# Key norms read off the gram's diagonal on GpSimd, with x loaded into the tile of the gated products and the gram's load issued later

## The chip, the cores and the metric

The kernel runs on one core of one Trainium2 chip. The metric is the time of one execution on the device, in microseconds.

## The reference

A gated delta rule over 16 heads of size 16, then a layer norm, a gated feed-forward network and another layer norm. Batch 8, length 2048, width 256, hidden 768.

```python
x_act = jnp.tanh(x)
static_out = jnp.einsum('bld,ed->ble', x_act, W)
q = k = to_heads(x_act); v = to_heads(static_out)
# per head and token, with lam = sigmoid(lam_logit), beta = eta * (1 - lam) / d:
S = lam * S
u = beta * (v_t - S^T k_t)
S = S + k_t u_t^T
o = S^T q_t
...
y = layernorm(static_out + o) * ln_gamma + ln_beta
x = layernorm(x + y)
x = layernorm(x + (silu(x @ wg.T) * (x @ wu.T)) @ wd.T)
```

Since q is k, the output of a token holds the term (k_t . k_t) u_t: the squared norm of each head's key times the update. These squared norms, one for each token and head, are what the text calls the key norms. They are scaled and shifted (beta times a constant, minus a constant) into the tile nb.

## The kernel before

The 2048 tokens of each batch row are cut into 32 chunks of 64 tokens (NS = 32). A chunk holds 4 windows (NW = 4) of 16 tokens (C = 16); with the 8 batch rows a window fills 128 partitions. The recurrence over the state runs window by window. Within a window it is done with matrices: the rest R = V - K S, then the update U = T R with T the inverse of a triangular matrix made from the gram K K^T, then the new state from K^T U. Each window is therefore a chain of three matmul groups (`pe_products`, line 182) with short VectorE and ScalarE steps between them: L361, L366, L372 make the rest, L377 and L382 the update, L388, L393, L399 the state.

The order of all work is written by hand: each engine has one step function (`pe_step`, `dve_step`, `act_step`, `pool_step`, `sp_step`) that is called with s = -3 to 34, and each engine executes its list strictly in order, waiting on semaphores. Step s holds four chunks at different stages: the recurrence of chunk s; gram, inverse and static output of chunk s+1; the load, tanh and transposes of chunk s+2; the norms of chunk s-1 and the feed-forward of chunk s-2. What belongs to one step stands in all five lists, but SyncE (SP), which issues every DMA from one queue, works through its list some half a step behind the others: its step s ends in the middle of the other engines' step s+1.

What the change touches, with the chunk's stages in order:

- `sp_load_x` (L994): four DMAs of 128 KB bring x of a chunk into the tile xa. It waits until the chunk before has left xa: `xtp` (transposed by TensorE) and `nr` (its squares summed by VectorE).
- `act_activate` (L677): tanh in place in xa, in ScalarE's list behind `act_mask_gram` and ahead of window 2's `act_update` (L664).
- The keys go to memory (`sp_store_keys`, two DMAs, L1003) and come back spread in two layouts: xb (`sp_spread_packed_keys`, eight DMAs, L1025) and E (`sp_spread_keys`, eight, L1016). The gram is made from both, window by window, into gs (ScalarE L715, VectorE L434).
- `sp_store_gram` (L1033) and `sp_load_gram` (L1040) carry the gram through memory, so that a partition holds one head of one batch row; the load waits for the store's landing (`gd`). VectorE multiplies it by nmask (`dve_mask_gram`, L428), ScalarE copies it to tt (`act_mask_gram`, L721), GpSimd writes ones on tt's diagonal (`pool_unit_diagonal`, L904), and VectorE inverts in 28 steps (L443, L451). nmask is zero on the diagonal and above.
- The inverse is split into two f16 parts by windows 0 and 1 (g = 0) and 2 and 3 (g = 1) (L731, L458), stored (L1047) and spread by eight DMAs for each g into tb (`sp_load_inverse`, L1059). k16, the scaled keys, go into kb by eight DMAs for each g (`sp_load_kb`, L1072).
- The norms: ScalarE squares xa (`act_square`, L682), VectorE sums over each head (`dve_square_sums`, L418) and scales (`dve_key_norms`, L423) into nb, which `pool_attention_out` (L912, L915, L920) reads a step later.
- hhi holds the six gated products of the feed-forward as f16; they are written at the end of one step and in the first third of the next, and read by `pe_down` until its `dn` in the middle of that step.

The SP list around the change is:

```python
store_gram(s + 2); load_gram(s + 2)
load_inverse(s + 1, 1)
load_x(s + 3)
store_out(s - 1)
# next sp_step
load_kb(s + 1, 0)
store_keys(s + 2, 0); store_keys(s + 2, 1)
spread_packed_keys(s + 2); spread_keys(s + 2)
store_inverse(s + 1, 0); load_residual(s)
store_inverse(s + 1, 1); load_inverse(s + 1, 0); load_kb(s + 1, 1)
```

Of the kernel before, what the change touches and what calls it, by code (L numbers as in the profile page):

```python
# [12 lines left out]
P = 128  # L13
B, L, D = 8, 2048, 256
H, DH = 16, 16
C = P // B
# [19 lines left out]
def build(nc, x, W, ln_gamma, ln_beta, eta, lam_logit, w_gate, w_up, w_down, out):  # L36
# [3 lines left out]
    with ctx:  # L40
# [3 lines left out]
        def sem(name):  # L44
# [24 lines left out]
        nb = sb("nb", [P, 2, NW, H])  # L69
# [5 lines left out]
        tt = sb("tt", [P, C, C, NW])  # L75
        tmp = gs[:, 0:C - 1, :, :]
# [33 lines left out]
        hlo = sb("hlo", [P, NHT, TOK], F16)  # L110
        pc = ctx.enter_context(nc.psum_tensor("pc", [P, 512], F32))
# [7 lines left out]
        scr_g = nc.dram_tensor("scr_g", [H, B, C, T], F32).ap()  # L119
        scr_t = nc.dram_tensor("scr_t", [2, H, B, C, T], F16).ap()  # L120
# [3 lines left out]
            sq=1, nr=1, nb=1, k16h=2, k16=2,  # L124
# [290 lines left out]
        def dve_square_sums(dve, q, p):  # L415
            dve.wait_ge(SEM["y1"], n_of("y1", q - 2))
            dve.wait_ge(SEM["sq"], n_of("sq", q))
            dve.tensor_reduce(nb[:, p, :, :], xa[:, :, :].rearrange("p n (h k) -> p n h k", h=H),  # L418
                              AX.X, ALU.add).then_inc(SEM["nr"], 1)

        def dve_key_norms(dve, q, p):
            dve.wait_ge(SEM["nr"], n_of("nr", q))
            dve.tensor_scalar(nb[:, p, :, :], nb[:, p, :, :], sc[:, BETAR:BETAR + 1], -0.5 / RS,  # L423
                              ALU.mult, ALU.add).then_inc(SEM["nb"], 1)

# [78 lines left out]
        def dve_step(dve, s, p):  # L504
# [10 lines left out]
            if live(s):  # L515
                dve_key_norms(dve, s, p)
                dve_store_inverse(dve, s, p, 1)
# [55 lines left out]
            if live(s + 1):  # L573
                dve_square_sums(dve, s + 1, 1 - p)
            if live(s):
# [99 lines left out]
        def act_activate(act, q, p):  # L675
            act.wait_ge(SEM["xin"], n_of("xin", q))
            act.activation(xa[:, :, :], xa[:, :, :], ACT.Tanh).then_inc(SEM["xa"], 1)  # L677

        def act_square(act, q, p):
            act.wait_ge(SEM["k16"], n_of("k16", q))  # L680
            act.wait_ge(SEM["xtp"], n_of("xtp", q))
            act.activation(xa[:, :, :], xa[:, :, :], ACT.Square).then_inc(SEM["sq"], 1)  # L682
# [56 lines left out]
        def act_variance(act, q, p, z, n):  # L739

            x_, to, nq, va = ((res, v[:, p], nq2, va2), (x1_of(q), v[:, 1 - p], nq3, va3))[z - 2]
            if n == 0:
                act.wait_ge(SEM[f"mq{z}"], n_of(f"mq{z}", q))
                if z == 2 and q == NS - 1:
                    act.wait_ge(SEM["nr"], n_of("nr", q))
# [39 lines left out]
        def act_step(act, s, p):  # L785
# [43 lines left out]
            if live(s + 1):  # L829
                act_square(act, s + 1, 1 - p)  # L830
# [75 lines left out]

        def pool_attention_out(pool, q, p, w):
            pool.wait_ge(SEM["u"], n_of("u", q, w + 1))
            if w == 0:
# [7 lines left out]
                               nb[:, p, w, :, None].to_broadcast([P, H, DH]), ALU.mult)\  # L917
# [37 lines left out]
        def pool_step(pool, s, p):  # L955
# [6 lines left out]
            if live(s):  # L962
                pool_unit_diagonal(pool, s, p)
            if live(s - 2):
                pool_bias(pool, s - 2, p, 2)
            if live(s - 1):
                pool_attention_out(pool, s - 1, 1 - p, 2)
# [20 lines left out]

        def sp_load_x(sp, q, p):
            sp.wait_ge(SEM["xtp"], n_of("xtp", q - 1))  # L990
            sp.sem_inc(s_hop, 1)
            sp.wait_ge(SEM["nr"], n_of("nr", q - 1))
            for n in range(NW):
                sp.dma_start(xa[:, n, :], x[:, q * T + n * C:q * T + (n + 1) * C, :]).then_inc(SEM["xin"], 16)  # L994
# [41 lines left out]
        def sp_load_gram(sp, q, p):  # L1036
            sp.wait_ge(SEM["gd"], n_of("gd", q))
            sp.sem_inc(s_hop, 1)
            sp.wait_ge(SEM["tf"], n_of("tf", q - 1))
            sp.dma_start(gh[:, :, :, :].rearrange("p i j n -> p (i j n)"),  # L1040
                         scr_g.rearrange("h b i t -> (h b) (i t)")).then_inc(SEM["gh"], 16)

# [49 lines left out]
        def sp_step(sp, s, p):  # L1092
            if live(s + 1):
                sp_load_kb(sp, s + 1, 1 - p, 0)
            if later(s + 2):
                sp_store_keys(sp, s + 2, p, 0)
                sp_store_keys(sp, s + 2, p, 1)
# [10 lines left out]
            if live(s + 2):  # L1108
                sp_store_gram(sp, s + 2, p)
                sp_load_gram(sp, s + 2, p)  # L1110
            if live(s + 1):
                sp_load_inverse(sp, s + 1, 1 - p, 1)
            if later(s + 3):
                sp_load_x(sp, s + 3, 1 - p)
            if live(s - 1):
# [30 lines left out]
        N_SETUP = 1 + 8 + 2 * C + 7 + 1 + (C - 1)  # L1146

        @block.sync
        def _(eng):
            bc = lambda a, n: a.rearrange("(o n) -> o n", o=1).to_broadcast([P, n])  # L1150
            sp_load_x(eng, 0, 0)
# [57 lines left out]
        def _(eng):  # L1209
# [23 lines left out]
            flat = nmask[:, :, :].rearrange("p i j -> p (i j)")  # L1233
            for d in range(1, C):
# [68 lines left out]
```

## Time and profile before

| | us |
|---|---|
| median of 3 runs | 1711.97 |
| lowest and highest run | 1702.58, 1717.01 |
| the profiled execution: its own time | 1699.24 |
| the profiled execution: its span | 1697.4 |
| busy: TensorE 80%, VectorE 80%, ScalarE 66%, GpSimd 50% of the span | 1362.5, 1352.3, 1115.9, 842.8 |

The span runs from the first to the last instruction of the profiled execution. Its mean granted TensorE clock was 0.881 of full speed. A busy share is a mean over all stages: here every engine is idle for part of each step while it waits for another, so the shares say little about which wait sets the length of a step.

### The profile page before, as it was taken

The numbers are of one execution on the slowest core, as the hardware profiler recorded it, in microseconds if no ns is written. First come the engines' busy times: TensorE is split into PE (matmuls) and PEld (weight loads), VectorE is DVE, ScalarE is ACT, GpSimd is POOL, SyncE is SP. The second block draws the span as 40 slices with busy tenths as digits, with TensorE's granted clock in tenths as the row PEclk, the third lists the DMA queues.
The fourth block names the chain that finished last, engine by engine and source line by source line (L and its number), as shares of the span: only waits on it lengthen the run. The fifth ranks groups of instructions, "written<-read, shape, count | busy, mean of one in ns | idle before, by whom it ended". The sixth has DMA issues, their size and how long they took to land.

```text
span 1697.4 us, 53741 instructions
## 1 busy us (share of the span) xinstructions
PE 1362.5 (80%) x21032; PEld 1062.5 (63%) x21032; DVE 1352.3 (80%) x3461; ACT 1115.9 (66%) x2357; POOL 842.8 (50%) x1106
## 2 busy tenths in 40 slices
PE   4357888888888888888888888887888888888764
PEld 3345676666666666666666666666666666666542
DVE  5588888888888888888888888888788788888841
ACT  3335777667767776676777677766667677676544
POOL 6124455555544655454455555445555544555542
PEclk9557889989989998898899899898999899899877
DMA  4556445565655555566455566654565555455200
GB/s 121 118 109 119 106 122 121 119 124 114 130 118 120 122 122 116 114 123 130 110 120 119 120 125 117 125 116 115 115 116 121 114 131 117 118 117 120 52 23 25
DMA packets 701325, 190.98 MB, mean 113 GB/s; under 512 B 620944, under 2 KB 688528, under 8 KB 701072
## 3 DMA queue, kind: packets, MB, share of 16 engines
q1 hardware_dynamic: 701072, 187.56, 52.1%
q8 instruction: 165, 2.70, 0.7%
q14 instruction: 88, 0.72, 0.1%
HBM read 103.55 MB, written 67.11 MB: 101 GB/s over the span
## 4 chain that ended last, share of the span: by engine, by line
DVE 29%; SPq 18%; PE 16%; DMA 13%; issue 12%; ACT 8%; POOL 4%; ACTq 0%; POOLq 0%; DVEq 0%
SPq L1059 8%; DMA xa<-L_attn_x 6%; PE pc L182 6%; DMA scr_g<-gs 5%; PE pg L253 4%; DVE tt L451 4%; SPq L1072 4%; PE pu L253 4%; DVE gs L443 3%; DVE gate L495 3%; SPq L994 3%; DVE xt L406 2%; DVE x1lo L488 2%; DVE U L382 2%; DVE R L377 2%
## 5 line engine op out<-in xcount | busy, mean ns | idle before, releaser
L953 POOL TENSOR_TENSOR hlo<-gate,hhi 128x512 f16<-128x512 f32 x192 | 264.0, 1385 | 357.0 <-ACT hhi L783 354.9
L182 PE MATMUL pc<-R,tb 128*128 128x32 f16 x4096 | 158.1, 186 | 119.3 <-DVE R L372 117.3
L182 PEld LDWEIGHTS pc<-R,tb 128*128 128x128 f16 x4096 | 146.7, 118 | 139.8 <-DVE R L372 137.7
L182 PE MATMUL pc<-U,kb 128*128 128x32 f16 x4096 | 158.9, 188 | 85.3 <-DVE U L382 85.1
L182 PEld LDWEIGHTS pc<-U,kb 128*128 128x128 f16 x4096 | 146.9, 118 | 114.7 <-DVE U L382 114.6
L182 PEld LDWEIGHTS pc<-S,e 128*128 128x128 f16 x4096 | 150.1, 118 | 67.9 <-DVE S L399 64.4
L182 PE MATMUL pc<-S,e 128*128 128x32 f16 x4096 | 157.1, 186 | 41.5 <-DVE S L399 41.4
L279 PE MATMUL pd<-wd_t,hhi 128*128 128x256 f16 x768 | 174.5, 274 | 7.5 <-POOL hlo L953 5.1
L279 PE MATMUL pd<-wd_t,hlo 128*128 128x256 f16 x768 | 174.1, 274 | 0.0
L216 PEld LDWEIGHTS pf<-xb,e 128*128 128x128 f16 x4096 | 153.8, 118 | 31.5 <-DMA e<-scr_x 16.3
L216 PE MATMUL pf<-xb,e 128*128 128x32 f16 x4096 | 156.3, 191 | 17.5 <-DMA e<-scr_x 15.9
L495 DVE SCALAR_TENSOR_TENSOR gate<-pu,gate 128x512 f32<-128x512 f32 x192 | 129.0, 685 | 48.0 <-ACT gate L777 35.1
L443 DVE TENSOR_TENSOR gs<-tt,gh 128x56 f32<-128x56 f32 (+6 forms) x448 | 145.2, 324 | 23.6 <-ACT tt L721 14.6
L253 PE MATMUL pg<-x1hi,wg_t 128*128 128x512 f16 x384 | 154.2, 402 | 11.5 <-DVE x1lo L488 10.0
L777 ACT ACTIVATE gate<-pg 128x512 f32<-128x512 f32 x192 | 113.7, 593 | 75.5 <-PE pg L253 71.8
L451 DVE TENSOR_TENSOR tt<-tt,gs 128x56 f32<-128x56 f32 (+6 forms) x448 | 146.4, 327 | 12.1
L783 ACT ACTIVATE hhi<-gate 128x512 f16<-128x512 f32 x192 | 119.7, 629 | 49.8 <-DVE gate L495 48.1
L253 PE MATMUL pg<-x1lo,wg_t 128*128 128x512 f16 x384 | 152.1, 396 | 0.0
L253 PE MATMUL pu<-x1lo,wu_t 128*128 128x512 f16 x384 | 149.0, 388 | 0.0
L253 PE MATMUL pu<-x1hi,wu_t 128*128 128x512 f16 x384 | 149.0, 388 | 0.0
L227 PE MATMUL pf<-w_t,xt 128*128 128x256 f16 x1024 | 139.4, 282 | 0.4 <-DVE gs L434 0.4
L434 DVE SCALAR_TENSOR_TENSOR gs<-pf,gs 128x256 f32<-128x256 f32 x128 | 85.0, 664 | 62.2 <-ACT gs L715 62.0
(132 smaller groups left out, 3222.4 us busy)
## 6 DMA issues: line engine op xcount, KB each, us to landing
xa<-L_attn_x SPq DMA_DIRECT2D x128, 128.0 KB
scr_x<-xt SPq DMA_DIRECT2D x64, 256.0 KB, 2.1
xb<-scr_x SPq DMA_DIRECT2D x256, 64.0 KB, 2.9
e<-scr_x SPq DMA_DIRECT2D x256, 64.0 KB, 3.7
scr_g<-gs SPq DMA_DIRECT2D x32, 512.0 KB, 3.5
gh<-scr_g SPq DMA_DIRECT2D x32, 512.0 KB, 3.3
kb<-k SPq DMA_DIRECT2D x512, 32.0 KB, 2.3
scr_t<-t SPq DMA_DIRECT2D x64, 256.0 KB, 3.6
```

The lines of the kernel that those rows point to most:

```text
L182: last = pe.matmul(pc2[:, :, cols], stationary(h, a), moving[:, :, cols], start=a == 0, stop=a == 1)
L216: last = pe.matmul(pf[n % 2][:, 2 * h * C:2 * (h + 1) * C].rearrange("p (z j) -> p z j", z=2), E[p][:, ez, h, :, :, n].rearrange("p b i -> ...
L227: last = pe.matmul(pf[g][:, (n % 2) * D:(n % 2 + 1) * D], xt[:, half, xz, :, :, n].rearrange("p b i -> p (b i)"), w_t[:, half, wz, :], sta ...
L253: last = pe.matmul(bank[:, :], wt[:, half, t * P:(t + 1) * P], xp[:, half, :], start=half + part == 0, stop=half + part == 2)
L279: last = pe.matmul(pd[:, (n % 2) * D:(n % 2 + 1) * D], hp[:, t, n * P:(n + 1) * P], wd_t[:, t, :], start=n % 2 + t + part == 0, stop=n % 2 ...
L443: dve.tensor_tensor(tmp[:, m, 0:C - 1 - j, :], tt[:, m, j:j + 1, :].to_broadcast([P, j, C - 1 - j, NW]), gh[:, i, j, :][:, None].to_broadc ...
L451: dve.tensor_tensor(tt[:, m, i, :], tt[:, m, i, :], tmp[:, m, 0:C - 1 - j, :], ALU.add)\
L495: dve.scalar_tensor_tensor(gate[:, k, :], pu[k][:, :], W_SCALE * HS / XS, gate[:, k, :], ALU.mult, ALU.mult).then_inc(SEM["h"], 1)
L777: act.activation(gate[:, k, :], pg[k][:, :], ACT.Silu, scale=W_SCALE / XS).then_inc(SEM["si"], 1)
L783: act.activation(hhi[:, t, :], gate[:, t % 2, :], ACT.Copy).then_inc(SEM["hh"], 1)
L953: pool.tensor_tensor(hlo[:, t, :], gate[:, t % 2, :], hhi[:, t, :], ALU.subtract).then_inc(SEM["hl"], 1)
L1059: sp.dma_start(tb[C * b:C * (b + 1), g, :, b].rearrange("j h i z m -> j h (i z m)"), scr_t[g, :, b].rearrange("h j t -> j h t")).then_inc( ...
```

## The change

The squares, their sums and their scaling leave ScalarE and VectorE. nmask gets ones on its diagonal, so that the masked gram keeps the squared norms there; GpSimd reads the diagonal, scales it into a new tile nd, and two DMAs turn it through memory into the layout of nb, which now holds four chunks. x of chunks 1 to 31 is loaded into the first four of hhi's six products (seen as f32), and the tanh reads from there and writes xa. The gram's load moves behind the inverse's second spread and the load of x in SP's list. `pool_unit_diagonal` moves behind `pool_bias` in GpSimd's.

```diff
-        nb = sb("nb", [P, 2, NW, H])
+        nb = sb("nb", [P, 4, H, NW])
+        nd = sb("nd", [P, C, NW])
+        xs = hhi[:, 0:4, :].rearrange("p t n -> p (t n)").bitcast(F32).rearrange("p (n d) -> p n d", n=NW)
+        scr_n = nc.dram_tensor("scr_n", [H, B, C, NW], F32).ap()
...
-        def dve_square_sums(dve, q, p): ...
-        def dve_key_norms(dve, q, p): ...
-        def act_square(act, q, p): ...
...
         def act_activate(act, q, p):
             act.wait_ge(SEM["xin"], n_of("xin", q))
-            act.activation(xa[:, :, :], xa[:, :, :], ACT.Tanh).then_inc(SEM["xa"], 1)
+            act.wait_ge(SEM["xtp"], n_of("xtp", q - 1))
+            act.wait_ge(SEM["k16"], n_of("k16", q - 1))
+            act.activation(xa[:, :, :], (xs if q else xa)[:, :, :], ACT.Tanh).then_inc(SEM["xa"], 1)
...
+        def pool_key_norms(pool, q, p):
+            pool.wait_ge(SEM["tf"], n_of("tf", q, 1))
+            pool.wait_ge(SEM["kd"], n_of("kd", q - 1))
+            pool.tensor_scalar(nd[:, :, :], gh[:, :, :, :].rearrange("p i j n -> p (i j) n")[:, 0:C * C:C + 1, :],
+                               sc[:, BETAR:BETAR + 1], -0.5 / RS, ALU.mult, ALU.add).then_inc(SEM["nd"], 1)
...
                 pool_attention_out(pool, s - 1, 1 - p, 1)
             if live(s):
+                pool_key_norms(pool, s, p)
+            if live(s - 2):
+                pool_bias(pool, s - 2, p, 2)
+            if live(s):
                 pool_unit_diagonal(pool, s, p)
-            if live(s - 2):
-                pool_bias(pool, s - 2, p, 2)
...
         def sp_load_x(sp, q, p):
-            sp.wait_ge(SEM["xtp"], n_of("xtp", q - 1))
+            if q == 1:
+                sp.wait_ge(s_ps, NJ)
+                sp.sem_inc(s_hop, 1)
+            sp.wait_ge(SEM["dn"], n_of("dn", q - 4))
             sp.sem_inc(s_hop, 1)
-            sp.wait_ge(SEM["nr"], n_of("nr", q - 1))
+            sp.wait_ge(SEM["xa"], n_of("xa", q - 1))
             for n in range(NW):
-                sp.dma_start(xa[:, n, :], ...
+                sp.dma_start(xs[:, n, :], ...
...
         def sp_load_gram(sp, q, p):
...
             sp.wait_ge(SEM["tf"], n_of("tf", q - 1))
+            sp.sem_inc(s_hop, 1)
+            sp.wait_ge(SEM["nd"], n_of("nd", q - 1))
...
+        def sp_store_norms(sp, q, p):
+            sp.wait_ge(SEM["nd"], n_of("nd", q))
+            sp.sem_inc(s_hop, 1)
+            sp.wait_ge(SEM["nb"], n_of("nb", q - 1))
+            sp.dma_start(scr_n.rearrange("h b i n -> (h b) (i n)"), nd[:, :, :].rearrange("p i n -> p (i n)"))\
+              .then_inc(SEM["kd"], 16)
+
+        def sp_load_norms(sp, q, p):
+            sp.wait_ge(SEM["kd"], n_of("kd", q))
+            sp.sem_inc(s_hop, 1)
+            sp.wait_ge(SEM["y1"], n_of("y1", q - 4))
+            sp.dma_start(nb[:, q % 4], scr_n.rearrange("h b i n -> (b i) h n")).then_inc(SEM["nb"], 16)
...
             if live(s + 1):
                 sp_load_kb(sp, s + 1, 1 - p, 0)
+                sp_store_norms(sp, s + 1, 1 - p)
             if later(s + 2):
                 sp_store_keys(sp, s + 2, p, 0)
+            if live(s + 1):
+                sp_load_norms(sp, s + 1, 1 - p)
+            if later(s + 2):
                 sp_store_keys(sp, s + 2, p, 1)
...
                 sp_store_gram(sp, s + 2, p)
-                sp_load_gram(sp, s + 2, p)
             if live(s + 1):
                 sp_load_inverse(sp, s + 1, 1 - p, 1)
             if later(s + 3):
                 sp_load_x(sp, s + 3, 1 - p)
+            if live(s + 2):
+                sp_load_gram(sp, s + 2, p)
             if live(s - 1):
                 sp_store_out(sp, s - 1, 1 - p)
...
             link(eng.memset(nmask[:, :, :], 0.0))
             flat = nmask[:, :, :].rearrange("p i j -> p (i j)")
+            link(eng.memset(flat[:, 0:C * C:C + 1], 1.0))
```

## Rows read from the trace of the kernel before

**Rows 1.** The page's chain of work that ended last, by line.
```profile
SPq L1059 8%; DMA xa<-L_attn_x 6%; PE pc L182 6%; DMA scr_g<-gs 5%; PE pg L253 4%; DVE tt L451 4%; SPq L1072 4%; PE pu L253 4%; DVE gs L443 3%; DVE gate L495 3%; SPq L994 3%; DVE xt L406 2%; DVE x1lo L488 2%; DVE U L382 2%; DVE R L377 2%
```

**Rows 2.** Timeline of SP's queue: start us, us, issues, number merged.
```profile
864.56 0.39 SPq L1033 DMA_DIRECT2D scr_g<-gs  x1
...
868.40 3.81 SPq L1059 DMA_DIRECT2D tb<-scr_t  x8
...
912.86 0.53 SPq L1033 DMA_DIRECT2D scr_g<-gs  x1
...
916.87 4.88 SPq L1059 DMA_DIRECT2D tb<-scr_t  x8
921.87 2.68 SPq L994 DMA_DIRECT2D xa<-L_attn_x  x4
...
927.45 5.92 SPq L1072 DMA_DIRECT2D kb<-k  x8
933.97 1.20 SPq L1003 DMA_DIRECT2D scr_x<-xt  x2
936.91 5.54 SPq L1025 DMA_DIRECT2D xb<-scr_x  x8
...
961.75 0.53 SPq L1033 DMA_DIRECT2D scr_g<-gs  x1
```

**Rows 3.** Waits of SP's queue: us in total, times, longest us.
```profile
SPq L1038 <- DMA scr_g<-gs: 104.5, 32, 4.5
...
SPq L1045 <- DVE t L458: 33.4, 28, 13.5
SPq L1030 <- DVE gs L434: 24.4, 15, 14.5
```

**Rows 4.** Waits in total: engine, line, waited for: us, times, longest us.
```profile
ACT xa L677 <- DMA xa<-L_attn_x: 18.7, 20, 2.0
```

**Rows 5.** Timeline of VectorE; idle time before, and its releaser, in brackets.
```profile
876.11 1.22 DVE L428 TENSOR_TENSOR gh<-gh,nmask 128x1024 f32<-128x1024 f32 x1
...
916.13 0.42 DVE L501 SCALAR_TENSOR_TENSOR xr<-pd,xr 128x256 f32<-128x256 f32 x1
...
918.58 1.21 DVE L418 TENSOR_REDUCE nb<-xa 128x64 f32<-128x1024 f32 x1
920.40 0.42 DVE L377 SCALAR_TENSOR_TENSOR R<-pc,U 128x256 f32<-128x256 f32 x1 [0.61 <-ACT U L664]
...
924.01 1.22 DVE L428 TENSOR_TENSOR gh<-gh,nmask 128x1024 f32<-128x1024 f32 x1
925.42 0.48 DVE L361 SCALAR_TENSOR_TENSOR R<-pc,dcol,v 128x256 f32<-128x256 f32 x1 [0.20 <-PE pc L182]
...
929.38 0.42 DVE L377 SCALAR_TENSOR_TENSOR R<-pc,U 128x256 f32<-128x256 f32 x1 [0.96 <-ACT U L664]
...
949.17 0.24 DVE L423 TENSOR_SCALAR nb<-nb,sc 128x64 f32<-128x64 f32 x1
```

**Rows 6.** Timeline of ScalarE.
```profile
917.22 0.50 ACT L749 ACTIVATE v<-xr,nq 128x256 f32<-128x256 f32 x1
...
928.02 1.06 ACT L677 ACTIVATE xa<-xa 128x1024 f32<-128x1024 f32 x1 [0.71 <-DMA xa<-L_attn_x]
```

**Rows 7.** Timeline of GpSimd.
```profile
916.98 0.20 POOL L928 TENSOR_TENSOR nq<-sm,by_16d 128x4 f32<-128x4 f32 x1 [4.23 <-DVE xr L501]
...
927.39 0.32 POOL L904 TENSOR_TENSOR tt<-powers 128x64 f32<-128x64 f32 x1 [3.70 <-ACT tt L721]
```

**Rows 8.** The gram's load (tile gh): issue to landing, all 32.
```profile
DMA to landing us min/median/max: 3.2/3.3/4.3
```

**Rows 9.** The page's DMA issues: count, KB each, median us to landing.
```profile
scr_x<-xt SPq DMA_DIRECT2D x64, 256.0 KB, 2.1
...
scr_g<-gs SPq DMA_DIRECT2D x32, 512.0 KB, 3.5
...
kb<-k SPq DMA_DIRECT2D x512, 32.0 KB, 2.3
```

More of the change, by code:

```diff
@@ L123, in build @@
             xin=64, xa=1, xtp=2, xth=2, xt=2,
-            sq=1, nr=1, nb=1, k16h=2, k16=2,
+            nd=1, kd=16, nb=16, k16h=2, k16=2,
             xtd=32, e=128, xb=128, vp=2, v=2,
@@ L413, in dve_scale_keys @@
                .then_inc(SEM["k16"], 1)
[L415 to L424, printed above, removed]
         def dve_mask_gram(dve, q, p):
@@ L515, in dve_step @@
             if live(s):
-                dve_key_norms(dve, s, p)
                 dve_store_inverse(dve, s, p, 1)
@@ L572, in dve_step @@
                 dve_rest_low(dve, s, p, 1)
-            if live(s + 1):
-                dve_square_sums(dve, s + 1, 1 - p)
-            if live(s):
                 dve_update_high(dve, s, p, 1)
@@ L676, in act_activate @@
             act.wait_ge(SEM["xin"], n_of("xin", q))
-            act.activation(xa[:, :, :], xa[:, :, :], ACT.Tanh).then_inc(SEM["xa"], 1)
[L679 to L682, printed above, removed]
+            act.wait_ge(SEM["xtp"], n_of("xtp", q - 1))
+            act.wait_ge(SEM["k16"], n_of("k16", q - 1))
+            act.activation(xa[:, :, :], (xs if q else xa)[:, :, :], ACT.Tanh).then_inc(SEM["xa"], 1)
         def act_transpose_keys(act, q, p, half):
@@ L744, in act_variance @@
                 if z == 2 and q == NS - 1:
-                    act.wait_ge(SEM["nr"], n_of("nr", q))
+                    act.wait_ge(SEM["xtp"], n_of("xtp", q))
                     act.wait_ge(SEM["k16"], n_of("k16", q))
@@ L828, in act_step @@
                 act_decay(act, s, p, 1)
-            if live(s + 1):
-                act_square(act, s + 1, 1 - p)
             if live(s - 2):
@@ L916, in pool_attention_out @@
                                bu[:, :].rearrange("p (h d) -> p h d", h=H),
-                               nb[:, p, w, :, None].to_broadcast([P, H, DH]), ALU.mult)\
+                               nb[:, q % 4, :, w, None].to_broadcast([P, H, DH]), ALU.mult)\
                 .then_inc(SEM["y1"], 1)
@@ L962, in pool_step @@
             if live(s):
-                pool_unit_diagonal(pool, s, p)
+                pool_key_norms(pool, s, p)
             if live(s - 2):
                 pool_bias(pool, s - 2, p, 2)
+            if live(s):
+                pool_unit_diagonal(pool, s, p)
             if live(s - 1):
@@ L986, in pool_step, with sp_load_first_x @@
                 pool_mean(pool, s - 1, 1 - p, 2)
+        def sp_load_first_x(sp):
+            for n in range(NW):
+                sp.dma_start(xa[:, n, :], x[:, n * C:(n + 1) * C, :]).then_inc(SEM["xin"], 16)
         def sp_load_x(sp, q, p):
-            sp.wait_ge(SEM["xtp"], n_of("xtp", q - 1))
+            if q == 1:
+                sp.wait_ge(s_ps, NJ)
+                sp.sem_inc(s_hop, 1)
+            sp.wait_ge(SEM["dn"], n_of("dn", q - 4))
             sp.sem_inc(s_hop, 1)
-            sp.wait_ge(SEM["nr"], n_of("nr", q - 1))
+            sp.wait_ge(SEM["xa"], n_of("xa", q - 1))
             for n in range(NW):
-                sp.dma_start(xa[:, n, :], x[:, q * T + n * C:q * T + (n + 1) * C, :]).then_inc(SEM["xin"], 16)
+                sp.dma_start(xs[:, n, :], x[:, q * T + n * C:q * T + (n + 1) * C, :]).then_inc(SEM["xin"], 16)
         def sp_store_keys(sp, q, p, half):
@@ L1145, in build @@
         NJ = len(jobs)
-        N_SETUP = 1 + 8 + 2 * C + 7 + 1 + (C - 1)
+        N_SETUP = 1 + 8 + 2 * C + 7 + 2 + (C - 1)
         @block.sync
@@ L1150, in _ @@
             bc = lambda a, n: a.rearrange("(o n) -> o n", o=1).to_broadcast([P, n])
-            sp_load_x(eng, 0, 0)
+            sp_load_first_x(eng)
             eng.dma_start(sc[:, ETA:ETA + 1], eta.to_broadcast([P, 1])).then_inc(s_ldc, 16)
```

## The prediction

> **What bounds the kernel now.** Every engine idles for part of each step, so I began with the chain of waits by line [rows 1]. The reader is to see that it does not stay on one engine: SP's issues (L1059, L1072, L994), the landing of x and the landing of the gram's store stand in it beside VectorE and TensorE. Next the timeline of SP's queue over one step [rows 2]. The gram's store was issued at 912.86 and again at 961.75, so a step takes 48.9 us, and there are some 30 full steps. Between the gram's store and its load SP stands still for the store's landing (104.5 us in 32 waits [rows 3], 3.3 us a step), and x is issued only behind that wait and the inverse's second spread: at 921.87, 9.0 us after the gram's store. Then the waits in total: ScalarE sat idle before the tanh for x's landing in 20 of 32 steps, 18.7 us in all [rows 4]. The tanh stands ahead of window 2's update in ScalarE's list, so this idle time reaches the recurrence: VectorE waited 0.61 us for ScalarE in window 1's update (L377 at 920.40) and 0.96 us in window 2's (at 929.38) [rows 5].
>
> **The loop that matters.** Three things run around once per step: the recurrence with VectorE's other work, SP's queue, and the crossings between them. One crossing is gram store, x, tanh, update of window 2. The other is gram store, gram load, mask (L428), rest of window 2. Before, the second has room: the mask ran at 924.01 straight behind VectorE's other work, without a wait for its data [rows 5]. The change shortens the first crossing and lengthens the second.
>
> **Part 1: x earlier (gain).** x now waits for `dn` two chunks back and the tanh before, not for xa to be free. VectorE used the last down products at 916.13 [rows 5], while SP comes to x only after the store and the eight spreads, 0.53 + 4.88 us after 912.86, so at 918.3: no wait there. x is issued 3.6 us earlier (921.87 to 918.3), more than the longest of the tanh's waits, 2.0 us [rows 4]. All 18.7 us of idle time go: **-18.7 us**; bounds 0 (something else late at once) and -18.7. What is late next is in part 4. The tanh's own 1.06 us stays where it is, behind ScalarE's copy of the masked gram.
>
> **Part 2: squares and sums away (near nothing).** VectorE's sum takes 1.21 us at 918.58 and ends at 919.79; VectorE then still idled 0.61 us until ScalarE's update at 920.40 [rows 5]. It lies wholly in the time that TensorE and ScalarE need between rest and update, so without it the wait becomes 1.8 us long. ScalarE's square stood ahead of a variance that began at 917.22 [rows 6]; GpSimd's scaled mean, for which that waits, ended at 917.18 [rows 7]. So 0 there too. If that cover were gone (no wait behind either) the pair would be worth over 30 us; nothing in the rows offers that.
>
> **Part 3: the scaling away (small gain).** `dve_key_norms` takes 0.24 us at 949.17 [rows 5] between two multiplications and the split of the inverse for which SP waits. Instructions there overlap by some 0.1 us, which leaves 0.15 a step, 4.5 us. Some of it is lost in later waits: **-4 us**, bounds 0 and -7 (0.24 by 30).
>
> **Part 4: the gram's load later (cost).** After the change SP issues, behind the gram's store: eight spreads and four loads of x, then the gram. By the rows 0.53 + 4.88 + 2.68 us and about 0.3 between them: 8.4 us after the store, and 7.3 with the 3.81 us that the eight took at 868.40 [rows 2]; I take 7.8. In place of the wait for the store's landing, over by then, it has the wait for the old norms, over for long. The load lands 3.2 to 4.3 us after its issue [rows 8]; behind x in the same queue I take 3.8. So it lands 11.6 us after the store (bounds 10.5 and 12.7). VectorE came to the mask 11.55 us after the store in one step (876.11 less 864.56) and 11.15 in the next (924.01 less 912.86) [rows 2, 5]. The mask is thus late by about 0.25 us on average (bounds 0 and 1.5). Queued behind it on VectorE are the rest of window 2 and all after it; that rest had waited 0.20 us for TensorE [rows 5], which absorbs the first part. Who else waits: ScalarE's copy of the gram, then the tanh and the update of window 2. I count 0.1 us a step here before part 5.
>
> A rule bears on the landing. The Trainium skill, page "DMA: Bandwidth & Descriptors", section "Queues, rings and completion order", says that a DMA's semaphore increment lands only after every earlier write of that DMA engine. By it the gram's landing cannot overtake that of x; the upper end of the landings above would be the usual one, and the mask about 0.5 us a step later than I take. No row here puts a large load directly behind x, so the trace doesn't decide it.
>
> **Part 5: the norms on GpSimd and through memory (cost).** GpSimd's new instruction has the shape of the diagonal's, 0.32 us [rows 7], and stands in an idle time of 3.70 us ahead of it; the diagonal itself is wanted only some 15 us later. On SP two DMAs are added. The store comes behind kb's first eight, which ended at 933.37, and will come about 3 us earlier since the wait of 3.3 is gone [rows 2, 3]; so it stands in front of the keys' store at 933.97 without delaying it, and has landed by then. The load of the norms stands between the two key stores. It moves 32 KB in 2048 pieces of 16 bytes. Price from both sides: a DMA of 32 KB in 256 pieces lands after 2.3 us; the gram's store, 2048 pieces of 256 bytes, after 3.5, and its load, the same bytes in 128 pieces, after 3.3 [rows 8, 9]. So sixteen times the pieces cost 0.2 us there, and the norms' load should keep the queue for 0.1 to 1.5 us beyond its own issue of 0.4 to 0.5. The second key store, and with it the wait for its landing (933.97 to 936.91 [rows 2]), ends later by 0.4 to 1.8 us; I take **1.0**. All of SP's queue behind that moves: both spreads of the keys, then the stores of the inverse. There SP waited for VectorE 27 times for 19.9 us without the longest (0.74 us each), and before the gram's store 14 times for 9.9 us [rows 3]. These waits absorb about two thirds; some 0.35 us a step reach the gram's store, and from there the mask, which with part 4 leaves no room. Parts 4 and 5 together: 0.1 + 0.3 = 0.4 us a step by 30: **+12 us**; bounds 0 and 1.4 a step, +42.
>
> **Part 6: the edges.** One more memset in the setup, a few tenths. At the start x of chunk 1 no longer waits for the gram store's landing; the tail has no load of x. Within 1 us: 0, bounds -3 and +1.
>
> **Sum.** -18.7 - 4 + 12 = **-11 us**. Against the profiled execution, 1699.24 us of its own time (1697.4 of span), that is 1688; this execution was 0.7% below the median of the runs, 1711.97. The same 0.6% on the median gives **1702 us**.
>
> **Rivals.**
> The gap is closed in full. SP no longer stands 3.3 us a step, so it is ahead at every later wait, the norms' load costs nearly nothing, and the mask is never late: -18.7 - 7 - 3, say -29, 1683 us. For it: the small price of pieces in the rows, and 11.55 against 11.6 us is a draw. Against: SP's gain is ahead of the keys' store, where it waits for VectorE anyway, so it isn't carried further. Chance 0.25.
>
> The gram's load takes x's place as what is late. It lands 12.7 us after the store; the mask is late by 1.2 us less 0.2 of room, and with 0.3 from part 5 that is 1.3 us a step, 39 us, against 18.7 + 4 saved: +16, 1728 us. It decides in the other direction from a lateness of 0.75 us a step on. For it: gram and x share a queue, and the load of x stands directly ahead. This is also where the skill's rule above would lead: 0.5 us a step more than I take is +15 on -11, so +4, and the rest needs slow spreads. Chance 0.17.
>
> The 16-byte pieces are slow. If the norms' load holds the queue for 3 us and not one, the key spreads start 3 us later, SP's waits absorb 0.9 of that, and the rest goes to the spread of the next inverse and to the gram's store: 2 us a step, 60 us less 23 saved: +37, 1749 us. The point from which it decides: 1.6 us of hold. Against: 2048 pieces of sixteen times the size land after 3.5 us all told. The same page of the Trainium skill says in its "Specifications" that writes below 512 bytes are read, modified and written; most DMAs here are below that already, so the trace has it in its prices. Chance 0.11.
>
> That the change doesn't do what it says: if `dn` were late x would be too. VectorE at 916.13 excludes it by 2 us.
>
> **How the numbers follow.** My forecast, 1692 to 1711, has 0.47; the rivals 0.25, 0.17 and 0.11. A change under 1% is about what a measurement of this kernel can't tell from none. The forecast's own spread crosses -1% (1695): a fifth of it, and nearly all of the first rival, is faster by more: 0.10 + 0.24 = 0.34. Slower by over 1% (1729) are half of the second rival and nearly all of the third, 0.19. The rest, 0.47, is within 1%. The range that leaves out 2 in 10 runs from the first rival, with a few us below it for waits that shrink too, to between the second and the third: 1676 to 1738.
>
> **What would show it.** Right: no idle time before the tanh for x; the gram's store to its load 7.3 to 8.4 us; VectorE idle before L428 for the gram, some tenths a step; VectorE's idle time before window 1's update grown by 1.2 us. Part 5 is right if the key store to the first spread grows from 2.94 to about 4 us and SP's waits for VectorE shrink. Wrong: VectorE's wait at the mask over 1 us in most steps, or the norms' load landing after more than 4 us, or update 2 still late for a ScalarE instruction that I took for covered. A step that hardly changes although the tanh's wait is gone would mean that TensorE's work for the feed-forward set it all along.

## The result: 5.6% slower, and the profile after

The changed kernel takes 1806.95 us in the median, 1.0561 times the kernel before (95% interval 1.0513 to 1.0609). The forecast was 1702 us in a range of 1676 to 1738. The profiled execution has a span of 1805.7 us against 1697.4.

First the page's busy times and its chain of work, to be set beside [rows 1].

```profile
PE 1378.0 (76%) x21032; PEld 1068.9 (59%) x21032; DVE 1305.6 (72%) x3398; ACT 1084.0 (60%) x2325; POOL 842.4 (47%) x1138
...
SPq L1073 13%; DMA gh<-scr_g 11%; SPq L1086 5%; SPq L1024 5%; SPq L1015 5%; SPq L993 4%; DMA scr_x<-xt 4%; PE pg L256 3%; PE pu L256 2%; DMA scr_t<-t 2%; ACT v L734 2%; PE pc L185 2%; ACT tt L706 2%; POOL rs L930 2%; ACT xa L667 2%
```

VectorE and ScalarE do what they were meant to do: 46.7 and 31.9 us less work. The span grew all the same. The landing of x is gone from the chain; the landing of the gram's load (11%) has come in its place, and SP's own issues. The waits by engine and the DMA issues name the place. The columns are those of rows 3 and 9.

```profile
DVE gh L420 <- DMA gh<-scr_g: 113.9, 31, 9.2
```

```profile
scr_x<-xt SPq DMA_DIRECT2D x64, 256.0 KB, 3.1
...
gh<-scr_g SPq DMA_DIRECT2D x32, 512.0 KB, 6.1
```

In the kernel before VectorE waited for the gram once, 3.6 us at the start. Now it does in 31 of 32 steps, for 3.7 us each. The gram's load takes 6.1 us from issue to landing, where it took 3.3 [rows 8], and the store of the keys 3.1 where it took 2.1 [rows 9]. One step of SP's queue, to be read beside [rows 2], and VectorE in it:

```profile
931.77 0.40 SPq L1032 DMA_DIRECT2D scr_g<-gs  x1
932.29 4.58 SPq L1073 DMA_DIRECT2D tb<-scr_t  x8
936.98 2.66 SPq L993 DMA_DIRECT2D hhi<-L_attn_x  x4
939.83 0.35 SPq L1041 DMA_DIRECT2D gh<-scr_g  x1
941.61 2.89 SPq L1104 DMA_DIRECT2D y_out<-xr  x4
944.62 5.32 SPq L1086 DMA_DIRECT2D kb<-k  x8
950.05 0.53 SPq L1048 DMA_DIRECT2D scr_n<-nd  x1
955.58 0.38 SPq L1002 DMA_DIRECT2D scr_x<-xt  x1
956.07 0.40 SPq L1055 DMA_DIRECT2D nb<-scr_n  x1
956.58 1.10 SPq L1002 DMA_DIRECT2D scr_x<-xt  x1
959.78 4.61 SPq L1024 DMA_DIRECT2D xb<-scr_x  x8
```

```profile
939.72 0.42 DVE L380 SCALAR_TENSOR_TENSOR R<-pc,U 128x256 f32<-128x256 f32 x1 [1.75 <-ACT U L652]
...
946.53 1.23 DVE L420 TENSOR_TENSOR gh<-gh,nmask 128x1024 f32<-128x1024 f32 x1 [3.12 <-DMA gh<-scr_g]
...
950.90 0.42 DVE L380 SCALAR_TENSOR_TENSOR R<-pc,U 128x256 f32<-128x256 f32 x1 [0.24 <-ACT U L652]
```

In this step the gram's load is issued 8.1 us after its store, within the forecast's 7.3 to 8.4. It lands 6.7 us later, with the mask at 14.8 us after the store in place of 11.15 and 11.55. But the step is one of the short ones. The spreads, which take 4.58 us here, take 5.3 us in the median of the full steps, and the load is issued 9.0 us after the store; the mask comes 15.2 us after it, straight behind the landing. Two steps on:

```profile
1035.52 0.53 SPq L1032 DMA_DIRECT2D scr_g<-gs  x1
...
1041.81 2.66 SPq L993 DMA_DIRECT2D hhi<-L_attn_x  x4
1044.66 0.34 SPq L1041 DMA_DIRECT2D gh<-scr_g  x1
```

The two updates show what became of the work saved: VectorE's wait before window 1's update is 1.75 us, was 0.61 [rows 5] (the sum had lain in it), and before window 2's it is 0.24, was 0.96 (the tanh no longer waits for x). Behind the norms' load the second key store takes 1.10 us to issue, and the first spread starts 4.2 us after the first key store, was 2.94 [rows 2].

The mean granted clock of TensorE was 0.844 of full speed, 0.881 before, and its busy time grew by 15.5 us. In the runs below it is mostly lower where the time is longer (0.826 in e11, the slowest, and 0.899 in e6). No run holds it fixed, so what part of a difference in time it makes is not shown.

### The profile page after: what moved, and what is told of

Same layout as the page of the kernel before. It is cut to its first block, busy times and chain, and to the rows that moved or that the text cites. A ratio compares the mean times of both kernels' runs of the same rounds, so it can differ in the third digit from the quotient of the medians.

```text
span 1805.7 us, 53837 instructions
## 1 busy us (share of the span) xinstructions
PE 1378.0 (76%) x21032; PEld 1068.9 (59%) x21032; DVE 1305.6 (72%) x3398; ACT 1084.0 (60%) x2325; POOL 842.4 (47%) x1138
## 4 chain that ended last, share of the span: by engine, by line
SPq 37%; DMA 19%; issue 11%; DVE 9%; ACT 9%; PE 9%; POOL 6%; ACTq 0%; POOLq 0%; DVEq 0%
SPq L1073 13%; DMA gh<-scr_g 11%; SPq L1086 5%; SPq L1024 5%; SPq L1015 5%; SPq L993 4%; DMA scr_x<-xt 4%; PE pg L256 3%; PE pu L256 2%; DMA scr_t<-t 2%; ACT v L734 2%; PE pc L185 2%; ACT tt L706 2%; POOL rs L930 2%; ACT xa L667 2%
## 5 line engine op out<-in xcount | busy, mean ns | idle before, releaser
L942 POOL TENSOR_TENSOR hlo<-gate,hhi 128x512 f16<-128x512 f32 x192 | 255.9, 1341 | 377.6 <-ACT hhi L768 376.3
L647 ACT ACTIVATE R<-R 128x256 f16<-128x256 f32 x128 | 52.8, 413 | 166.0 <-DVE R L364 166.0
```

What stands on the lines that cost most here:

```text
L942: pool.tensor_tensor(hlo[:, t, :], gate[:, t % 2, :], hhi[:, t, :], ALU.subtract).then_inc(SEM["hl"], 1)
```

## The experiments

Two suspects stood after the traces: the gram's load behind x, and the norms' load in front of the keys. The first four kernels part them. Ratios are to the kernel before on the same chip, with 95% intervals.

**e1, the gram's load ahead of x.** The changed kernel with one swap in SP's list.

```diff
             if live(s + 1):
                 sp_load_inverse(sp, s + 1, 1 - p, 1)
-            if later(s + 3):
-                sp_load_x(sp, s + 3, 1 - p)
             if live(s + 2):
                 sp_load_gram(sp, s + 2, p)
+            if later(s + 3):
+                sp_load_x(sp, s + 3, 1 - p)
```

> The changed kernel with one swap: the gram's load issued behind the inverse's second spread and ahead of x, not behind x. Theory A (the gram's load lands late because x's four loads stand directly ahead of it in the same queue: 6.1 us from issue to landing in the changed kernel against 3.3 before): the load lands after 3.3 to 3.8 us, is issued 5.3 to 6 us after the gram's store, VectorE's wait before the mask (113.9 us) falls below 5 us, x still comes before the tanh wants it; the time is 1690 +- 12, below the kernel before. Theory B (the norms' way through memory delays SP's queue by its two DMAs, and that set the time): the time stays above 1770. Theory C (the landing is slow because of the inverse's eight spreads that also stand ahead now): the load lands after more than 5 us, the time stays above 1750.

Measured: 1712.79 us, ratio 1.0025 (1.0010 to 1.0041). The gram's load lands after 3.5 us, x is there for the tanh, and both waits are those of the start alone:

```profile
DVE gh L420 <- DMA gh<-scr_g: 6.2, 1, 6.2
ACT xa L667 <- DMA hhi<-L_attn_x: 1.1, 1, 1.1
```

So 5.4 of the 5.6% are the place of one DMA. But the time is 23 us above what theory A gave: the gain of the early x is there (18.7 us of waiting gone) and something takes it back.

**e2, the gram's load at its old place.** The changed kernel, with this swap.

```diff
                 sp_store_gram(sp, s + 2, p)
+                sp_load_gram(sp, s + 2, p)
             if live(s + 1):
                 sp_load_inverse(sp, s + 1, 1 - p, 1)
             if later(s + 3):
                 sp_load_x(sp, s + 3, 1 - p)
-            if live(s + 2):
-                sp_load_gram(sp, s + 2, p)
```

> The changed kernel with the gram's load back at its old place, directly behind the gram's store and its landing. Theory A: landing after 3.3 us, no wait before the mask; SP's wait of 3.3 us a step for the store's landing is back and x is issued 8 to 9 us after the store as before, so the tanh waits for it as before: 1705 +- 12. Theory B: stays above 1770, since both DMAs of the norms are still there. Theory C: as A.

Measured: 1746.08 us, 1.0212 (1.0180 to 1.0243). The load lands after 3.5 us, SP waits 103.1 us for the store's landing again, and the time is 41 us above theory A's. So a loss of 2.1% is left that is not the gram's; in e1, where the wait for the store's landing is filled, it was 0.25%.

**e3, the order alone.** The kernel before with x, then the gram's load, behind the inverse's second spread.

```diff
                 sp_store_gram(sp, s + 2, p)
-                sp_load_gram(sp, s + 2, p)
             if live(s + 1):
                 sp_load_inverse(sp, s + 1, 1 - p, 1)
             if later(s + 3):
                 sp_load_x(sp, s + 3, 1 - p)
+            if live(s + 2):
+                sp_load_gram(sp, s + 2, p)
```

> The kernel before with the new order of SP's list alone: inverse's second spread, x, then the gram's load. Norms stay on ScalarE and VectorE, x goes into xa. Theory A: the gram's load lands after about 6 us, VectorE waits 3 to 4 us a step before the mask, and the whole loss is here: 1795 to 1830. Theory B: within 1% of the kernel before, 1700 to 1725.

Measured: 1836.09 us, 1.0738 (1.0697 to 1.0780). It is worse than the whole change. x here also waits for VectorE's sums (46.1 us of SP's queue) and the gram's load behind it is issued later (10.1 us after the store in the median, against 9.0):

```profile
DVE gh L428 <- DMA gh<-scr_g: 156.1, 31, 9.1
```

```profile
gh<-scr_g SPq DMA_DIRECT2D x32, 512.0 KB, 6.5
```

**e4, x by batch rows.** The changed kernel, order kept.

```diff
-            act.wait_ge(SEM["xin"], n_of("xin", q))
+            act.wait_ge(SEM["xin"], 64 + 128 * q)
...
-            for n in range(NW):
-                sp.dma_start(xs[:, n, :], x[:, q * T + n * C:q * T + (n + 1) * C, :]).then_inc(SEM["xin"], 16)
+            for b in range(B):
+                sp.dma_start(xs[C * b:C * (b + 1)], x[b, q * T:(q + 1) * T, :].rearrange("(n i) d -> i n d", n=NW))\
+                  .then_inc(SEM["xin"], 16)
```

> The changed kernel, order kept, with x loaded by eight DMAs of 64 KB, one for each batch row (16 partitions x 4 windows of 1 KB), in place of four of 128 KB (one for each window: 8 batch rows x 16 tokens). Same bytes, same pieces of 1 KB. If each of the four is spread over only part of the DMA engines, because its outermost dimension in memory is 8, the gram's pieces on these engines stand behind 64 pieces of x and not 32: with eight DMAs the outermost dimension is 16, and the gram's load should land after 4 to 4.6 us in place of 6.1, though issued 1.7 us later for four more issues: VectorE's wait at the mask hardly changes, 1790 to 1815. If it is the amount of x alone that stands ahead, the landing stays at 6 us and the time rises to about 1850.

Measured: 1783.14 us, 1.0431 (1.0399 to 1.0464). The page's DMA issues and SP's queue:

```profile
gh<-scr_g SPq DMA_DIRECT2D x32, 512.0 KB, 3.6
```

```profile
917.18 0.40 SPq L1033 DMA_DIRECT2D scr_g<-gs  x1
917.71 4.61 SPq L1074 DMA_DIRECT2D tb<-scr_t  x8
922.43 5.00 SPq L993 DMA_DIRECT2D hhi<-L_attn_x  x8
927.62 0.34 SPq L1042 DMA_DIRECT2D gh<-scr_g  x1
```

The same 512 KB in the same pieces of 1 KB stand ahead, and the landing is 3.6 us and not 6.1. So it isn't the amount of x alone that delays the gram, it is how x's DMAs are cut. The eight issues take 5.00 us in this step (3.8 in the median) where the four took 2.66, and the gram's load is issued 10.0 us after its store in the median, against 9.0. That takes back part of what the shorter landing gives. The time, 1783, is below the 1790 to 1815 that I expected.

**e11, x by windows and half the batch rows.** The control to e4: eight DMAs of 64 KB with 64 pieces of 1 KB each there too, only over another part of x.

```diff
-            act.wait_ge(SEM["xin"], n_of("xin", q))
+            act.wait_ge(SEM["xin"], 64 + 128 * q)
...
             for n in range(NW):
-                sp.dma_start(xs[:, n, :], x[:, q * T + n * C:q * T + (n + 1) * C, :]).then_inc(SEM["xin"], 16)
+                for b in (0, B // 2):
+                    sp.dma_start(xs[C * b:C * (b + B // 2), n, :],
+                                 x[b:b + B // 2, q * T + n * C:q * T + (n + 1) * C, :]).then_inc(SEM["xin"], 16)
```

> The changed kernel, order kept, with x loaded by eight DMAs of 64 KB as in e4, 64 pieces of 1 KB each as in e4, but each over 4 batch rows x 16 tokens of one window, so that the outermost dimension in memory is 4 and not 16. If a DMA is spread over as many engines as its outermost dimension allows (8 in the changed kernel with a landing of the gram of 6.1 us, 16 in e4 with 3.6), x now stands on 4 engines with 128 pieces each: the gram's load lands after 9 to 12 us, and the time is 1900 or more. If e4's landing was shorter because of the smaller DMAs or their later issue, it stays at 3.6 here and the time is that of e4, 1783.

Measured: 1871.69 us, 1.0934 (1.0901 to 1.0968).

```profile
gh<-scr_g SPq DMA_DIRECT2D x32, 512.0 KB, 5.8
```

```profile
959.25 0.46 SPq L1034 DMA_DIRECT2D scr_g<-gs  x1
959.84 4.41 SPq L1075 DMA_DIRECT2D tb<-scr_t  x8
964.37 4.77 SPq L994 DMA_DIRECT2D hhi<-L_attn_x  x8
969.33 0.34 SPq L1043 DMA_DIRECT2D gh<-scr_g  x1
```

With equal count, size and pieces, the landing is 5.8 us against e4's 3.6, and the time 89 us longer. In the two steps shown the load is issued within 0.4 us of the same place after the store; in the median it is 10.9 us in e11 and 10.0 in e4. So of the 2.8 us by which the mask comes later in e11 (16.7 us after the store against 13.9), 2.1 are the landing and 0.9 the issue. The shape decides. The size was wrong: I expected 9 to 12 us of landing.

The Trainium skill, page "DMA: Bandwidth & Descriptors", section "Why a DMA increments its semaphore by 16 and not by 1", says that a DMA runs on the largest number of engines up to 16 that divides the slowest dimension of both sides: 16 for e4, 8 for the changed kernel, 4 here. The traces agree. They hold each increment that a DMA made to its semaphore. x's semaphore got 16 increments from each load in e4. In the changed kernel it got 9, one of them 1.1 us after the issue and eight later, and in e11 5, one early and four later.

The gram's load made 16 increments in every kernel, and they show what stood ahead of it. The table has the medians over the steps, in us after the load's issue. Its last column is the last increment of the x issued ahead.

| | engines with x, by x's increments | the gram's increments | last of x |
|---|---|---|---|
| e1, x behind the gram | | 16 at 2.9 to 3.5 | |
| e4 | 16 | 16 at 2.9 to 3.6 | 1.5 |
| changed kernel | 8 | 8 at 3.3 to 3.7, 8 at 4.2 to 6.1 | 4.8 |
| e11 | 4 | 12 at 3.3 to 4.0, 4 at 5.1 to 5.8 | 4.5 |

Where x is on 8 engines, 8 of the gram's increments are late, and where it is on 4, 4 are. On all 16 it is gone 1.5 us after the gram's issue and costs the landing almost nothing. In both kernels with late increments the gram lands 1.3 us after the last of x in the median. That fits why 4 engines delay it no more than 8: x was issued over 4.8 us in e11 and over 2.7 in the changed kernel, and its end came at nearly the same time after the gram's issue.

**e5, the norms alone.** The kernel before with GpSimd's norms and their two DMAs; x goes into xa, SP's order is the old one. Against e2 that is:

```diff
-            if q == 1:
-                sp.wait_ge(s_ps, NJ)
-                sp.sem_inc(s_hop, 1)
-            sp.wait_ge(SEM["dn"], n_of("dn", q - 4))
+            sp.wait_ge(SEM["xtp"], n_of("xtp", q - 1))
             sp.sem_inc(s_hop, 1)
-            sp.wait_ge(SEM["xa"], n_of("xa", q - 1))
+            sp.wait_ge(SEM["k16"], n_of("k16", q - 1))
             for n in range(NW):
-                sp.dma_start(xs[:, n, :], ...
+                sp.dma_start(xa[:, n, :], ...
...
-            act.wait_ge(SEM["xtp"], n_of("xtp", q - 1))
-            act.wait_ge(SEM["k16"], n_of("k16", q - 1))
-            act.activation(xa[:, :, :], (xs if q else xa)[:, :, :], ACT.Tanh).then_inc(SEM["xa"], 1)
+            act.activation(xa[:, :, :], xa[:, :, :], ACT.Tanh).then_inc(SEM["xa"], 1)
```

> The kernel before with the norms' part of the change alone (GpSimd, and the two DMAs through memory); x goes into xa and SP's order is the old one, the gram's load directly behind its store. Theory N (the load of the norms holds the queue in front of the second key store, so that the wait for the keys' landing grows by 1.4 us a step as it did in e1, of which the kernel before can absorb 0.8): 1.5% to 2.5% slower than before, 1733 to 1750, the key store's landing 3.1 us. Theory G (the norms off ScalarE and VectorE are a gain of their own, 2.7 us a step less work): 1% or more faster than before.

Measured: 1746.66 us, 1.0208 (1.0186 to 1.0230), the same as e2. The store of the keys lands after 3.1 us, and the tanh waits longer for x than before:

```profile
ACT xa L665 <- DMA xa<-L_attn_x: 31.0, 27, 2.7
```

The time and the landing are theory N's: the loss of 37 us is the norms' own, though 80 us of work went off ScalarE and VectorE. What in them costs it e7 and e9 tell.

**e6, early x with the old norms.** e1's order and x's new tile, the norms on ScalarE and VectorE.

```diff
-                sp_load_gram(sp, s + 2, p)
             if live(s + 1):
                 sp_load_inverse(sp, s + 1, 1 - p, 1)
+            if live(s + 2):
+                sp_load_gram(sp, s + 2, p)
...
+            act.wait_ge(SEM["nr"], n_of("nr", q - 1))
-            act.activation(xa[:, :, :], xa[:, :, :], ACT.Tanh).then_inc(SEM["xa"], 1)
+            act.activation(xa[:, :, :], (xs if q else xa)[:, :, :], ACT.Tanh).then_inc(SEM["xa"], 1)
...
-            sp.wait_ge(SEM["xtp"], n_of("xtp", q - 1))
+            sp.wait_ge(SEM["dn"], n_of("dn", q - 4))
             sp.sem_inc(s_hop, 1)
-            sp.wait_ge(SEM["nr"], n_of("nr", q - 1))
+            sp.wait_ge(SEM["xa"], n_of("xa", q - 1))
             for n in range(NW):
-                sp.dma_start(xa[:, n, :], ...
+                sp.dma_start(xs[:, n, :], ...
```

> The kernel before, norms on ScalarE and VectorE as there, with x loaded into the first four gated products, and SP's order store of the gram, inverse's second spread, load of the gram, x. Theory N: e1 lost its gain to the norms' DMAs alone; without them the tanh never waits for x, the mask is on time, and SP keeps its 0.8 us of room: 0.6 to 0.8 us a step less than before, 1.2% to 1.6% faster, 1680 to 1690. If something else eats e1's gain (the aliasing with the gated products, the mask just in time), it stays within 0.5% of before.

Measured: 1685.80 us, 0.9858 (0.9838 to 0.9878). The one wait of the tanh left is 1.0 us at the start.

**e8, the order with nothing else.** The kernel before with the gram's load behind the inverse's second spread; x follows, into xa.

```diff
                 sp_store_gram(sp, s + 2, p)
-                sp_load_gram(sp, s + 2, p)
             if live(s + 1):
                 sp_load_inverse(sp, s + 1, 1 - p, 1)
+            if live(s + 2):
+                sp_load_gram(sp, s + 2, p)
             if later(s + 3):
                 sp_load_x(sp, s + 3, 1 - p)
```

> The kernel before with one swap in SP's list: the inverse's second spread between the gram's store and its load; x behind both as before, into xa. Theory: the wait for the store's landing is filled by the spread, x is issued 6.5 us after the store and not 8.6 (its own wait for VectorE's sums at 6.9 can cost 0.5 us), which is still enough for the tanh: as e6, 1.0% to 1.5% faster than before, 1682 to 1692. If x's tile matters, e6 is faster than this one by 0.3% or more.

Measured: 1687.22 us, 0.9869 (0.9847 to 0.9891). x's tile is worth nothing that could be told: two moved lines give the whole gain. SP's waits show how: the wait for the gram store's landing, 104.5 us before [rows 3], is filled with issues; the wait for VectorE's sums that x now meets costs SP 28.2 us and the tanh only 1.3.

```profile
SPq L994 <- DVE nb L418: 28.2, 27, 1.9
...
SPq L1038 <- DMA scr_g<-gs: 2.9, 1, 2.9
```

**e7, the norms' load in wide pieces.** e1 with `scr_n` read back as it was stored.

```diff
-            sp.dma_start(nb[:, q % 4], scr_n.rearrange("h b i n -> (b i) h n")).then_inc(SEM["nb"], 16)
+            sp.dma_start(nb[:, q % 4].rearrange("p h n -> p (h n)"), scr_n.rearrange("h b i n -> (h b) (i n)")).then_inc(SEM["nb"], 16)
```

> e1 with the norms' load in 128 pieces of 256 bytes in place of 2048 of 16 bytes: the same 32 KB come back in the layout in which they were stored, so each partition of nb holds the norms of other tokens and heads than its own. Theory N with the pieces as its cause: the norms' load lands after 1.8 to 2.2 us in place of 3.1, the key store's landing falls from 3.1 to 2.3, SP's wait for it (68 us in all) to 56, and the time falls by 0.7 to 1 us a step against e1: 1680 to 1692. If the price is that of one more DMA with its issue and its wait whatever its pieces: 1705 to 1713, no change from e1.

Measured: 1694.28 us, 0.9907 (0.9885 to 0.9929), 1.2% below e1. From its DMA issues and SP's queue:

```profile
nb<-scr_n SPq DMA_DIRECT2D x32, 32.0 KB, 1.9
```

```profile
935.22 0.38 SPq L1002 DMA_DIRECT2D scr_x<-xt  x1
935.71 0.40 SPq L1055 DMA_DIRECT2D nb<-scr_n  x1
936.22 0.40 SPq L1002 DMA_DIRECT2D scr_x<-xt  x1
938.33 5.04 SPq L1024 DMA_DIRECT2D xb<-scr_x  x8
```

The second key store is issued in 0.40 us and not 1.10, it lands after 2.1 us, and the spread starts 3.1 us after the first store. 1.2 of the 1.7% between e1 and e6 are the 2048 pieces at this place in the queue. The rest, 0.5%, is left with two more DMAs in SP's list.

**e9 and e10, the norms' load elsewhere.** e1 with `sp_load_norms` behind the second key store (e9), or behind both spreads and the inverse's first store (e10). The first:

```diff
-            if live(s + 1):
-                sp_load_norms(sp, s + 1, 1 - p)
             if later(s + 2):
                 sp_store_keys(sp, s + 2, p, 1)
+            if live(s + 1):
+                sp_load_norms(sp, s + 1, 1 - p)
+            if later(s + 2):
                 sp_spread_packed_keys(sp, s + 2, p)
```

> e1 with the norms' load moved behind the second key store, so that its issue falls into SP's wait for the keys' landing. Theory N (the 2048 pieces cost what stands behind them in the queue): the key store's landing is 2.1 us again and the wait for it 56 us in all, but the first spread of the keys now stands behind the pieces and starts moving up to 1 us late: 1688 to 1700, between e1 (1.0025 of before) and e6 (0.986). If only the two more DMAs in SP's list counted, it would stay at e1's time.

Measured: 1686.64 us, 0.9861 (0.9835 to 0.9887), at the lower edge of what I expected. Its issue falls into SP's wait for the keys' landing, 46.5 us now, was 68.1 in e1:

```profile
929.18 1.23 SPq L1002 DMA_DIRECT2D scr_x<-xt  x2
930.51 0.40 SPq L1055 DMA_DIRECT2D nb<-scr_n  x1
932.31 5.32 SPq L1024 DMA_DIRECT2D xb<-scr_x  x8
```

The same two DMAs with the same pieces (the load still lands after 3.1 us) leave the time where e6 has it. So what e1 pays for the pieces and for the two DMAs is in the main the price of their place; a few us more or less could hide behind the work saved on the two engines (e13 below).

e10 has it here:

```diff
                 sp_store_inverse(sp, s + 1, 1 - p, 0)
+            if live(s + 1):
+                sp_load_norms(sp, s + 1, 1 - p)
             if live(s):
                 sp_load_residual(sp, s, p)
```

> e1 with the norms' load moved behind both spreads of the keys and the first store of the inverse, where nothing that is wanted soon stands behind it (the residual's load of x). Theory N: the key path is as in e6, SP has 0.5 us more of issue; with VectorE's 1.5 us and ScalarE's 1.1 us of norms gone: 1680 to 1690, as e6 or a little below. If the work taken off VectorE and ScalarE is worth anything, this is faster than e6 by 0.3% or more; I expect it is not.

Measured: 1717.63 us, 1.0050 (1.0029 to 1.0070). A miss. I had called the residual's load unimportant. In SP's queue it is held behind the pieces and takes 4.32 us to issue (3.85 in the median), where it takes 2.66 in the other kernels, and the spread of the inverse is behind it; TensorE then waits for that spread, 20.0 us in 18 steps against 2.0 us in all before.

```profile
955.93 0.38 SPq L1055 DMA_DIRECT2D nb<-scr_n  x1
956.36 4.32 SPq L1096 DMA_DIRECT2D res<-L_attn_x  x4
```

```profile
PE pc L185 <- DMA tb<-scr_t: 20.0, 18, 2.8
```

**e13, no norms at all.** e6 without the square, the sums and the scaling.

```diff
-            act.wait_ge(SEM["nr"], n_of("nr", q - 1))
+            act.wait_ge(SEM["xtp"], n_of("xtp", q - 1))
+            act.wait_ge(SEM["k16"], n_of("k16", q - 1))
...
-                act_square(act, s + 1, 1 - p)
...
-                dve_square_sums(dve, s + 1, 1 - p)
...
-                dve_key_norms(dve, s, p)
...
+            link(eng.memset(nb[:, :, :, :], -0.5 / RS))
```

> e6 with the norms left out: no square on ScalarE, no sums and no scaling on VectorE, nb a constant written once. Part 2 of the prediction (square and sums lie in waits) and part 3 (the scaling is worth 4 us): within 0.4% of e6, 1678 to 1687, VectorE's idle time before window 1's update grown by about 1.2 us. If the work taken off the two engines is worth what it takes (2.7 us a step), 1610 to 1640; then e9, which has it off too, pays as much again for its two DMAs.

Measured: 1684.62 us, 0.9830 (0.9795 to 0.9865). Against e6's 0.9858 that is 0.3%, some 5 us, and the two intervals overlap: taken together they leave anything from nothing to some 12 us. Yet ScalarE and VectorE do 72 us of work for the norms (29.4 and 42.5 less than in e6). VectorE's waits for ScalarE before the updates grow from 41.3 us in all in e6 to 76.9. One of them, before window 1's update:

```profile
911.96 0.42 DVE L378 SCALAR_TENSOR_TENSOR R<-pc,U 128x256 f32<-128x256 f32 x1 [1.75 <-ACT U L661]
```

## Why the prediction was wrong

The time, the range and the sign were wrong. By its own steps:

- **Part 4 failed: the gram's load behind x, its landing above all.** The landing was taken as 3.8 us with 4.3 as the end, from a row in which nothing large stood ahead. It is 6.1 behind x, and 3.5 as soon as x is behind it (e1). The issue was taken as 7.8 us after the store with 8.4 as the end; it is 9.0 in the median, since the eight spreads took 5.3 us and not 3.81 to 4.88. Together 3.5 us a step, 2.3 of them the landing: the gram lands 15.1 us after its store and not 11.6, and VectorE waits 3.7 us for it in nearly every step where the forecast had 0.25. The bound of the mask's lateness, 1.5 us, was no bound: the worst of 32 landings under one neighbour says nothing about another. e1 takes the 5.4% back by moving that one DMA, and e3 makes the loss with nothing but the order.
- **The rival that the gram takes x's place was the right mechanism, too small.** It gave 1.3 us a step and 1728 us. I had the rule on landings beside it and priced it at 0.5 us a step. It is borne out: in no step of the changed kernel, e4 or e11 did the gram land before the last of x. But that x would take until 4.8 us after the gram's issue I had not worked out, since I hadn't looked at the form of its loads. In e4, with the same bytes ahead, it takes 1.5 us, and an order of landings costs next to nothing.
- **Part 1 was right in its mechanism.** The tanh's wait for x went from 18.7 us to nothing. With the gram on time (e6, e8) the kernel gains 1.3 to 1.4%, 23 to 24 us, which is beyond the bound of 18.7. Where the other 5 us come from is open.
- **Parts 2 and 3 were right as far as can be told.** Square and sums lay in waits (0.61 us grew to 1.75), and all three operations together are worth some 5 us (e13 against e6), where the scaling had 4. The noise is larger than that.
- **Part 5's delay was nearly right, and its cost three times too small.** I took 1.0 us later for the first spread of the keys; it is 1.3. I let SP's waits for VectorE take up two thirds and charged 9 us. The norms alone cost 37 us (e5) and 28 on top of e6 (e1). The waits did shrink by about as much as I had let them: before the inverse's store from 33.2 us in 28 waits (e6) to 13.5 in 5 (e1), before the gram's store from 26.2 to 20.0, together 26 of some 40 us of delay. What the forecast left out are those who need the late spreads themselves, whatever SP does afterwards. TensorE waited for the second spread of the keys, from which the gram is made, 15 times in e1 and 4 times in e6. How the 28 us divide over such waits no run shows.

```profile
PEld pf L219 <- DMA e<-scr_x: 31.1, 15, 16.3
```

- **The rival of slow pieces** took 3 us of hold, and 1.6 us as the point from which it would decide. The norms' load lands after 3.1 us in all, and the spreads came 1.3 us late, so it stayed below its own point. It was not the cause of the result, but the pieces are 1.2% (e7 against e1).

The sum of what the runs show: order and early x -1.4% (e6), the norms' DMAs +1.7% (e1 less e6), the gram's load behind x +5.4% (changed less e1), together 5.6%. The shares hold for this order of steps; on the kernel before itself the norms cost 2.1% (e5). A version that beats the kernel before is e8, two moved lines; e6 and e9 are equal to it.

## What to carry to other kernels

When a DMA is moved behind another in the same queue, its old latency is no longer its price: work out what stands ahead and in what shape, above all the outermost dimension of each side, which decided here on how many engines the transfer ahead stood. A transfer's place is worth more than the instructions saved around it: here one DMA's place is worth 5.4%, another's 1.7% (e9 against e1), and 72 us of work on two engines some 0.3%, less than the noise. Fill the wait for a store's landing with small independent transfers, and put the load first among what follows (e8). And when a transfer comes later, count everyone who waits for it, not only the queue behind it.

## What the runs showed of the hardware that I had not expected

- 512 KB of x ahead of the gram's load delay its landing from 3.5 us (e1) to 6.1 when cut in four DMAs over 8 batch rows x 16 tokens, and to 3.6 when cut in eight over 16 tokens x 4 windows. Of the load's 16 increments 8 come late behind the first, none behind the second, and 4 behind eight loads over 4 batch rows x 16 tokens (e11).
- 2048 pieces of 16 bytes (32 KB) hold what is issued next: a store that issues in 0.40 us behind 128 pieces of 256 bytes needs 1.10 behind them, and the key stores land after 3.1 us, not 2.1. Issued into a wait (e9) the same pieces cost the kernel nothing that could be told.
